# Two-layer model on one core: 4-bit weights decoded through fp16 bit patterns, four VectorE operations a half chunk instead of seven

## The reference, cut to what matters

```python
NVFP4_LUT = [0.0, 0.5, 1.0, 1.5, 2.0, 3.0, 4.0, 6.0, 0.0, -0.5, -1.0, -1.5, -2.0, -3.0, -4.0, -6.0]

def dequant_nvfp4(W_packed, scales, block=32):
    low = W_packed & 15
    high = W_packed >> 4 & 15
    idx = jnp.stack([low, high], axis=-1).reshape(N, -1)
    vals = NVFP4_LUT[idx]
    return (vals.reshape(N, K // block, block) * scales[:, :, None]).reshape(N, K)

Wg, Wu, Wd = dequant(gate), dequant(up), dequant(down)      # 2048x256, 2048x256, 256x2048
gate, up = xt @ Wg.T, xt @ Wu.T
out = (gelu(gate) * up) @ Wd.T
```

## Time and profile before

| | |
|---|---|
| time, median of 3 runs | 801.63 us (797.67 to 805.33) |
| span of the profiled execution, first to last instruction | 801.1 us |
| time of the profiled execution beyond its span | not given apart; the span is 0.5 us from the median |
| PE busy | 620.3 us (77%) |
| DVE busy | 508.0 us (63%) |
| ACT, POOL busy | 283.7 us (35%), 249.7 us (31%) |
| moved by DMA | 62.83 MB, mean 78 GB/s |

### The profile page before, as it was taken

One profiled execution on the slowest core, in us unless ns is written; L12 is line 12 of the kernel. 1 busy time (PEld: TensorE's weight loads), 2 busy tenths in 40 slices (PEclk: granted clock), 3 DMA queues, 4 the chain that ended last, 5 costly groups with the idle time before them and its releaser, 6 DMA issues.

```text
span 801.1 us, 9617 instructions
## 1 busy us (share of the span) xinstructions
PE 620.3 (77%) x3248; PEld 469.8 (59%) x3248; DVE 508.0 (63%) x1121; ACT 283.7 (35%) x887; POOL 249.7 (31%) x288
## 2 busy tenths in 40 slices
PE   2997988740109789975385898898988789998996
PEld 0544766530008677763163665666666668887885
DVE  5547567833997536724677789889757636655444
ACT  2644544400103222332255665646646431111110
POOL 1228003275650000137545255251101126640000
PEclk9999999965559956987577999999999999999999
DMA  8900001049017996863112043150000000000000
GB/s 317 351 1 0 1 2 47 34 147 299 3 42 205 278 281 222 244 195 98 45 48 49 5 54 37 17 53 1 0 1 1 1 0 1 1 1 27 1 1 27
DMA packets 29808, 62.83 MB, mean 78 GB/s; under 512 B 5827, under 2 KB 13297, under 8 KB 29184
## 3 DMA queue, kind: packets, MB, share of 16 engines
q1 hardware_dynamic: 22336, 45.42, 18.1%
q0 software_dynamic: 7424, 16.80, 9.3%
HBM read 48.56 MB, written 17.83 MB: 83 GB/s over the span
## 4 chain that ended last, share of the span: by engine, by line
PE 53%; DVE 21%; issue 8%; ACT 8%; DMA 6%; POOL 2%; another core or an unknown queue 1%; SPq 1%; POOLq 0%; DVEq 0%; ACTq 0%
PE bank L1104 47%; DMA arena<-expert_in 4%; DVE arena L1054 2%; POOL expert_in L396 2%; ACT arena L594 2%; DVE arena L1013 2%; PE bank L1326 2%; PE bank L1444 1%; DVE arena L968 1%; DMA expert_out<-arena 1%; PE bank L1272 1%; ACT arena L612 1%; DMA arena<-in_wmod 1%; DVE arena L1002 1%
## 5 line engine op out<-in xcount | busy, mean ns | idle before, releaser
L1104 PE MATMUL bank<-arena 128*96 128x64 f32 (+9 forms) x2040 | 425.2, 367 | 64.0 <-issue 26.0
L1104 PEld LDWEIGHTS bank<-arena 128*128 128x128 f32 (+4 forms) x2040 | 295.3, 192 | 160.6 <-issue 100.9
L396 POOL DMA_INDIRECT expert_in<-arena x64 | 65.2, 1019 | 88.7 <-DVE arena L857 70.1
L410 POOL DMA_INDIRECT arena<-expert_out,arena x64 | 72.6, 1134 | 19.0 <-issue 18.5
L692 ACT ACTIVATE arena<-bank 128x512 f32<-128x512 f32 x32 | 19.1, 598 | 112.4 <-PE bank L1104 112.4
L1085 DVE TENSOR_TENSOR arena<-arena,bank 128x512 f32<-128x512 f32 x32 | 22.0, 687 | 56.1 <-ACT arena L692 56.1
L594 ACT ACTIVATE arena<-bank,arena 128x128 f32<-128x128 f32 x128 | 45.2, 383 | 25.2 <-DVE arena L1006 25.2
L1104 PE MATMUL bank<-h_hi,gu_hi 128*128 128x512 f32 x128 | 50.8, 397 | 0.5 <-ACT arena L695 0.5
L1104 PE MATMUL bank<-h_low,gu_hi 128*128 128x512 f32 x128 | 50.5, 394 | 0.0
L1104 PE MATMUL bank<-h_hi,low 128*128 128x512 f32 x128 | 50.1, 391 | 0.0
L434 POOL TENSOR_TENSOR low<-arena,gu_hi 128x128 fp32r<-128x128 f32 x64 | 29.7, 495 | 60.4 <-DVE dn_hi L1017 60.4
(11 more groups left out here) (200 smaller groups left out, 1024.2 us busy)
## 6 DMA issues: line engine op xcount, KB each, us to landing
arena<-in_wgu SPq DMA_DIRECT2D x32, 384.0 KB, 6.5
arena<-in_wd SPq DMA_DIRECT2D x32, 192.0 KB, 8.9
expert_in<-arena SPq DMA_DIRECT2D x1, 4096.0 KB, 23.9
arena<-expert_in SPq DMA_DIRECT2D x16, 256.0 KB, 7.2
expert_out<-arena POOLq DMA_DIRECT2D x16, 256.0 KB, 6.5
arena<-in_w SPq DMA_DIRECT2D x1, 2048.0 KB, 9.3
arena<-in_wmod SPq DMA_DIRECT2D x1, 1536.0 KB, 15.0
arena<-in_w_in SPq DMA_DIRECT2D x1, 1288.0 KB, 8.8
```

Of the source, the lines that this page charges most:

```text
L396: pool.indirect_dma_start(xin, bass.IndirectOffsetOnAxis(scatter8[:, t, k:k + 1], 0), h[:, t, :], None, bounds_check=SLOTS - 1, oob_is_err ...
L410: pool.indirect_dma_start(gath[t % 2][:, k, :], None, yex, bass.IndirectOffsetOnAxis(gather8[:, t, k:k + 1], 0), bounds_check=SLOTS - 1, o ...
L1104: return pe.matmul(o, lhsT, rhs, start=start, stop=stop, **kw)
```

## The change

`decode` builds each value from its bits. A code has three magnitude bits (two of exponent, one of mantissa) and a sign.

Before, the magnitude bits are shifted into a bf16 number and ORed with 0x3E00, so that no value is in the special lowest binade; two more operations (subtract a quarter and clamp at 0, add back) mend the two smallest values; then the sign is ORed in, and the last operation multiplies by 4 and by the scale.

Now the magnitude bits are shifted to bits 9 to 11 of an fp16 number, the sign to bit 15, and one OR joins them. Magnitudes 0 and 1 are the fp16 patterns 0x0000 and 0x0200, zero and a subnormal number; 2 to 7 are normal numbers of the two to three lowest binades. The last operation multiplies by 16384 in place of 4, reads fp16 in place of bf16, and writes float32 as before. The link after the first shift is gone and one stands after the second. Nothing else differs: not the buffers, the loads, the pace or any other engine.

```diff
-                vf, ff = nib[b][0].bitcast(bf16), nib[b][1].bitcast(bf16)
+                ff = nib[b][1].bitcast(f16)
 
                 if par == 0:
-                    link(dve.tensor_scalar(v, codes, 0x7, 6, ALU.bitwise_and, ALU.logical_shift_left))
-                    dve.tensor_scalar(s, codes, 0x8, 12, ALU.bitwise_and, ALU.logical_shift_left)
+                    dve.tensor_scalar(v, codes, 0x7, 9, ALU.bitwise_and, ALU.logical_shift_left)
+                    link(dve.tensor_scalar(s, codes, 0x8, 12, ALU.bitwise_and, ALU.logical_shift_left))
                 else:
-                    link(dve.tensor_scalar(v, codes, 0x70, 2, ALU.bitwise_and, ALU.logical_shift_left))
-                    dve.tensor_scalar(s, codes, 0x80, 8, ALU.bitwise_and, ALU.logical_shift_left)
-
-                link(dve.tensor_scalar(v, v, 0x3E00, None, ALU.bitwise_or))
-                link(dve.tensor_scalar(ff, vf, -0.25, 0.0, ALU.add, ALU.min))
-                link(dve.tensor_tensor(ff, ff, vf, ALU.add))
-                link(dve.tensor_tensor(f, f, s, ALU.bitwise_or))
+                    dve.tensor_scalar(v, codes, 0x70, 5, ALU.bitwise_and, ALU.logical_shift_left)
+                    link(dve.tensor_scalar(s, codes, 0x80, 8, ALU.bitwise_and, ALU.logical_shift_left))
+                link(dve.tensor_tensor(f, v, s, ALU.bitwise_or))
                 if which < 2:
                     dst = (wg_s, wu_s)[which][:, par, c * QC:(c + 1) * QC]
-                    last = dve.scalar_tensor_tensor(dst, ff, 4.0, sc[b], ALU.mult, ALU.mult)
+                    last = dve.scalar_tensor_tensor(dst, ff, 16384.0, sc[b], ALU.mult, ALU.mult)
                 else:
                     dst = wdn_s[:, 4 * c + par:4 * c + par + 3:2, :]
-                    last = dve.scalar_tensor_tensor(dst, ff.rearrange("p (a b) -> p a b", b=DM), 4.0,
+                    last = dve.scalar_tensor_tensor(dst, ff.rearrange("p (a b) -> p a b", b=DM), 16384.0,
                                                     sc[b].rearrange("p (a b) -> p a b", b=DM), ALU.mult, ALU.mult)
```

## The result

The changed kernel took 800.51 us (median of 12 runs, 797.55 to 808.14), the kernel before 798.55 us in its 12 runs of the same comparison (790.94 to 809.39). The ratio of the comparison is 1.0074, interval 1.004 to 1.0107. The forecast was 799.5 us with a range of 788 to 805, which holds the measured time. But it had the changed kernel 0.2 to 0.3% faster, and by this ratio it came out 0.7% slower.

A forecast was written before the change was run, and what follows sets the result against it. No engine was busy throughout; the expert stage was taken as bound by transfers, then by PE at the low clock. 801.1 - 1.2 - 0.6 = 799.3 us for the profiled execution, stated as 799.5, range 788 to 805.

The forecast's parts named there:

- The price of a half chunk: DVE's decoding: a half chunk falls from 3.09 to 1.99 us, saving 26 us of DVE's 508.
- Nearly all of those 26 us turn into idle time of DVE: Expert stage: DVE's saved decoding time mostly becomes waiting, since PE never stands idle for a product of DVE.
- How far does their landing move? ... I take 1.2: Rows PE awaits until 269.46: SP issues them 2.55 us sooner, they land 1.2 us sooner (0 to 2.55).
- the lower end: Landing of those rows moves by 0, since the DMA engines are full from 255 on.
- The argument from holes: Only time the DMA engines were not full after 250, 1.25 us, can be regained by earlier issues.
- the bytes ahead of these rows are the same: DMA queue ahead of those rows: an unchanged amount to move, given as reason for a landing shift of 0.
- The gap closes: 0.6 us: PE's 0.63 us wait at 329.66 vanishes because SP's codes go out 1.1 us sooner, gaining 0.6 us.
- The gap ahead of 284.00 ... stays about as long: PE's 2.56 us gap there moves 1.2 us earlier with its rows and keeps about its length.
- The clock as a rival with a chance of 0.20 and 0.06: Expert stage: altered gaps shorten PE's low clock, near 789 us (0.20), or lengthen it, 808.6 us (0.06).
- The slower rival: After the gap ahead of 269.46 the low clock lasts two more groups, costing 9.1 us: 808.6 us, chance 0.06.

The follow-up runs named there:

- e2: Changed kernel with shifts and OR left out, only the multiplication left in each half chunk (weights wrong): median 800.62 us, ratio 0.9966 to the kernel before.
- e5: The changed kernel unaltered, run a second time beside new runs of the kernel before: median 793.66 us, ratio 0.9926.
- first set: The first 12 runs of the changed kernel beside 12 of the kernel before: median 800.51 us, ratio 1.0074.
- e13: The changed kernel unaltered, run a third time beside the kernel before: median 798.94 us, ratio 0.9985.
- e9: Changed kernel with rows issued ahead of codes and ten late chunks loaded and decoded from group 5 on, two halves a group: median 789.31 us, ratio 0.9935.
- e10: Same order and late decoding as e9, but with the seven-operation decode of the kernel before: median 795.31 us, ratio 0.9989.
- e1: Changed kernel with three unused operations put back into every half chunk: median 800.37 us, ratio 1.0064 to the kernel before.
- e6: Kernel before with unused matmuls ahead of PE's waits for the rows of groups 6, 8, 9 and 10: median 796.87 us, ratio 0.9943.
- e7: Changed kernel with unused matmuls ahead of PE's waits for the rows of groups 6, 8, 9 and 10: median 797.25 us, ratio 0.9892.
- e8: Changed kernel with rows issued ahead of codes and unused matmuls ahead of groups 6, 8, 9 and 10: median 787.51 us in 6 runs, ratio 0.9839.
- e11: The same program as e8, run again against the kernel before: median 795.8 us in 12 runs, ratio 0.9945.

## Why the prediction was right or wrong

**The price of a half chunk** was right: 1.99 us from pieces; the trace has 1.97 linked and 1.86 unlinked, and the multiplication at 693 ns. (The pieces of the old half chunk add up to 3.08 us and not 3.06, which changes nothing.)

**"Nearly all of those 26 us turn into idle time of DVE"** was right: 25 us less busy, and no movement of the time that ± 5.9 us can tell even when e2 takes away 1.3 us more for each half.

**"How far does their landing move? ... I take 1.2"** is the step of the sum that failed. SP's issue moved by 2.0 to 2.3 us (2.55 forecast), the use of the rows in the profiled pair by 0 to 0.3 us: the lower end that the text gave, and not 1.2. Nor is the term a constant. In e5, the same program, the rows were there 2.1 us sooner than in the first set's execution, in e13 at the same time, so two numbers from one trace (a hole of 1.25 us, 0.63 us at the last gap) were added up where one execution differs from the next by more than their sum. The argument from holes has two weak places. The holes do not say that the earlier issues fill them; after the rows, SP's list waits for PE (`load_pair` waits for `down`), which would keep a hole open, though that was not tried by itself. And that "the bytes ahead of these rows are the same" is not borne out: what was moved from group 3 to group 6 was 4.9 to 5.5 MB in three executions. The page "DMA: Bandwidth & Descriptors" of the Trainium skill, section "Queues, rings and completion order", has a ring's descriptors taken in order. An issue 2.3 us earlier with next to nothing of it at the landing fits with that, but no run here tests the order itself.

**"The gap closes: 0.6 us"** has no counterpart: in the first profiled execution of the changed kernel PE was at the low clock at group 14 and had no gap to close. In e5 the clock was high there, and the gap is 1.96 us, longer and not closed.

**"The gap ahead of 284.00 ... stays about as long"** was wrong: it is gone, and gaps of 1.11 and 3.96 us stand ahead of groups 9 and 11. In e5 and e13, the same program, the gaps above 1 us are again elsewhere: ahead of groups 6, 13 and 14, and of 6 and 13.

**The clock as a rival with a chance of 0.20 and 0.06** was the larger error of method and, as far as the runs show, what decided the sign. It is not a case beside the sum but goes with every execution: the changed kernel's stage is 108, 122 and 124 us long with 37, 56 and 69 us at the low level, and the kernel before runs from 789 to 813 us, over ten times the sum. The three runs shown, 797.7 to 805.3, were taken as its width, and one execution's low stretch as its typical place. The page "TensorE: Matmul & The Clock Gate" of the Trainium skill, Part 1 (the HAM clock gate), says that sustained activity releases the throttle; these traces do not agree with it as it stands, since groups 11 to 14 of the changed kernel have PE recorded busy throughout at 0.50, 38.9 us long. The time came within 1.0 us of 799.5, which it owes to the median of before and not to the sum: 1.8 us are below what a dozen runs a side can tell (± 4.0 us), so neither the forecast's sign nor the measured one of the first set is borne out.

**The slower rival** gave the first set's sign but not its cause: the first fall did last longer (a group at 0.54 in place of a mean of 0.74), and the second came too, four groups long; yet in e5 and e13 the first low stretch lasts 29 and 20 us, in the first set 10, and the mean times of the three sets fall on both sides of before, so the first set's sign is a draw and no cost of the change.

What stays open: why the routing of the one profiled execution of before was 6 us late (its DVE waits 9.80 us on nothing that is recorded), what decides whether the low level lasts one group or five, and why the rows of group 6 came 2.1 us sooner in e5. None was tried. A true gain of 1 to 2 us by the change is neither shown nor ruled out.

## What to carry to other kernels

An engine that waits does not pay for being faster: ask first what a queue's earlier issue meets, and where the transfers are full, do not count on the landing to move with it. Where the clock falls after gaps, one profiled execution is one draw; compare many runs, and read their mean granted clock beside their times. A saving pays once the schedule is rebuilt to need it, as the four operations do when two half chunks must fit into one group (e9 against e10).

## What the runs showed of the hardware

- Over the 15 traces, each of the 15 gaps of PE above 2.5 us ahead of a group's transposes was followed by a stretch at 1.2 GHz, none of those under 1.6 us was, and of nine between (1.67 to 2.44 us), six were. How long the level then stayed, with PE busy, ranged from 3.4 us (before, group 6) to some 47 (e1, groups 6 to 10).
- Dense added matmuls (bf16, 128x512) ahead of the waits went with 2.4 GHz in all groups that had them (6, 8, 9, 10), in four traces of four (e6, e7, e8, e11). The low level came at groups without them: 13 in e6 and e7, 7 in e8, 7 and 14 in e11.
- VectorE reads subnormal fp16 at the price of bf16: 693 against 692 ns for 128x512 with a float32 scale.
